# One activation table for exponential and logarithm, Silu by ACT's own function in one block a phase, and the convolution in u's slot

## The reference, cut to what matters

```python
x = einsum('ed,bld->bel', in_proj_w, ctx)
u = silu(causal_conv4(x) + conv_b)                      # 4 taps per channel
x_dbl = einsum('ke,bel->bkl', x_proj_w, u)              # dt_lo (16), B (16), C (16)
delta = softplus(einsum('er,brl->bel', dt_proj_w, dt_lo) + dt_proj_b)
state = state * exp(delta_t * A) + (delta_t * u_t) * B_t   # for each position t
y_t = sum_n state[.., n] * C_t[n]
y = (y + D * u) * silu(layernorm(X))
X = X + tanh(g_xattn) * y
h = layernorm(X)
X = X + tanh(g_ffn) * (top-2 gates of softmax(h Wr); sum over slots of gate * (h U) V)
```

## Time and profile before

| what | before |
|---|---|
| median of 3 runs | 543.68 us (542.85 to 543.94) |
| the profiled execution's own time | 542.47 us |
| its span, first to last instruction | 540.7 us |
| PE busy | 490.6 us, 91% |
| DVE busy | 477.4 us, 88% |
| POOL busy | 457.8 us, 85% |
| ACT busy | 392.0 us, 73% |
| mean granted TensorE clock | 0.981 |

### The profile page before, as it was taken

The page is one execution under the profiler, slowest core; times in us unless marked ns, Lnnn a source line. Parts: engine busy times, 40 slices in busy tenths (PEclk is TensorE's granted clock), DMA queues, the critical chain, the costliest instruction groups (busy, mean ns, idle before and its releaser), DMA issues.

```text
span 540.7 us, 9249 instructions
## 1 busy us (share of the span) xinstructions
PE 490.6 (91%) x3032; PEld 368.2 (68%) x3032; DVE 477.4 (88%) x880; ACT 392.0 (73%) x702; POOL 457.8 (85%) x338
## 2 busy tenths in 40 slices
PE   9979888988687999999998999999999999899688
PEld 5568787868476777658676777667657766676654
DVE  3698999979899999889999999888988989999852
ACT  4567779576867678587967878577888888888542
POOL 0399999969999998979999999989798898987810
PEclk9979999999998899999999999999999999999799
DMA  5495001045320001065130000086100000000001
GB/s 135 154 370 220 0 2 32 10 154 191 128 78 2 1 0 59 2 211 222 59 99 1 19 2 21 4 269 235 44 15 8 19 22 19 2 20 21 1 20 39
DMA packets 18705, 39.37 MB, mean 73 GB/s; under 512 B 5585, under 2 KB 6353, under 8 KB 18658
## 3 DMA queue, kind: packets, MB, share of 16 engines
q1 hardware_dynamic: 18658, 38.79, 21.1%
HBM read 34.33 MB, written 4.46 MB: 72 GB/s over the span
## 4 chain that ended last, share of the span: by engine, by line
PE 60%; DVE 17%; ACT 13%; issue 8%; POOL 1%; DVEq 0%; ACTq 0%; POOLq 0%
PE p_s L754 14%; PE p_y L776 12%; DVE state L1260 9%; PE p_v L809 9%; PE p_f L800 7%; PE p_tr L721 4%; PE p_pr L684 3%; ACT da L1011 3%; PE p_pr L696 2%; PE p_pr L677 2%; PE p_f L789 2%; PE p_y L825 1%; DVE p_s L1260 1%; ACT p_s L1011 1%; PE p_y L765 1%
## 5 line engine op out<-in xcount | busy, mean ns | idle before, releaser
L573 POOL TENSOR_TENSOR state<-state,c_bc 128x1024 f32<-128x1024 f32 (+1 forms) x131 | 256.7, 1972 | 20.2 <-DVE state L1260 17.9
L754 PEld LDWEIGHTS p_s<-pair_b,du_t 128*128 128x128 f32 x1072 | 138.8, 197 | 45.2 <-issue 31.5
L754 PE MATMUL p_s<-pair_b,du_t 128*128 128x128 f32 x1072 | 152.7, 284 | 16.2 <-DVE state L1260 14.1
L776 PE MATMUL p_y<-ident,state 128*128 128x128 f32 x1024 | 149.3, 276 | 0.0
L558 POOL TENSOR_TENSOR dbu<-du,pair_b 128x1024 f32<-128x1024 f32 (+1 forms) x80 | 145.3, 1819 | 1.5 <-DVE p_s L1260 1.5
L1011 ACT ACTIVATE p_s<-delta,a_neg 128x512 f32<-128x512 f32 (+1 forms) x162 | 93.6, 581 | 70.0 <-DVE state L1260 34.2
L1260 DVE TENSOR_TENSOR_SCAN state<-da,p_s 128x512 f32<-128x512 f32 (+1 forms) x116 | 134.2, 1170 | 6.5 <-PE p_s L754 6.1
L776 PEld LDWEIGHTS p_y<-ident,state 128*128 128x128 f32 x1024 | 121.4, 144 | 23.7 <-issue 21.2
L1011 ACT ACTIVATE da<-delta,a_neg 128x512 f32<-128x512 f32 (+1 forms) x158 | 100.4, 648 | 18.6 <-DVE state L1260 18.2
L1260 DVE TENSOR_TENSOR_SCAN state<-p_s,dbu 128x512 f32<-128x512 f32 (+1 forms) x100 | 98.1, 996 | 3.5 <-POOL dbu L558 3.5
L800 PE MATMUL p_f<-u_sb,h_t 128*128 128x512 f32 x112 | 56.8, 610 | 1.2 <-DVE gw L1363 1.2
(11 more groups left out here) (182 smaller groups left out, 680.7 us busy)
## 6 DMA issues: line engine op xcount, KB each, us to landing
c_bc<-bc_rows SPq DMA_DIRECT2D x32, 512.0 KB, 5.4
pair_b<-bc_rows SPq DMA_DIRECT2D x16, 512.0 KB, 6.0
xs<-in_x SPq DMA_DIRECT2D x16, 256.0 KB, 4.1
out<-ot SPq DMA_DIRECT2D x14, 256.0 KB, 2.0
cx<-in_ctx_t SPq DMA_DIRECT2D x4, 512.0 KB, 3.7
u_sb<-in_u_w SPq DMA_DIRECT2D x1, 1024.0 KB, 14.1
v_sb<-in_v_w SPq DMA_DIRECT2D x1, 1024.0 KB, 15.6
w_in<-in_in_w_t SPq DMA_DIRECT2D x1, 384.0 KB, 4.7
```

Of the source, the lines that this page charges most:

```text
L573: eng.tensor_tensor(pair, pair, c_bc[:, 2 * p:2 * p + 2, c0:c0 + w], ALU.mult).then_inc(po_cs, 1)
L754: mm = eng.matmul(p_s[g % BANKS][:, t * P:(t + 1) * P], du_t[:, f % 2, t, :], diagonals_of(n // 2)[:, n % 2, c0 // P + t, :], start=(t == ...
L776: mm = eng.matmul(p_y[:, t, :], slot(NS * f + n)[:, t * P:(t + 1) * P], ident[:, :], is_transpose=True, start=False, stop=(n == NS - 1 and ...
```

## The change

- **z**: ACT computes silu(z) directly (`silu_z` on ACT), and the factor tanh(g_xattn) moves into the copy of the transposed result (`copy_sz`, now with a scale). DVE's `silu_z` and the halving in POOL's `scale_of_z` (6 small instructions, now 4) go.
- **u**: the convolution is built up in u's own slot (`conv_v`), a ring of 5 slots for 6, and ACT's Silu works in place. `tanh_v` on ACT and `silu_u` on DVE go, and DVE's two scalings of the tap weights by 0.5.
- **The block**: once a phase ACT loads Silu's table, makes the Silus and loads the set that has both Exp and Ln. It stands at n = 9, behind `skip`, in phases 12 to 19 only in the even ones and for two phases' z; in phases 2, 6 and 10 it stands at n = 15 and has two blocks of u, since the next phase needs them.
- **Opening**: the diagonal matrices of pairs 6, 7 and 0 of batch 0 move from POOL to ACT, four instructions of two tiles each per pair, behind the decays of n = 2 to 13 of phase 0. The fillers between the small projections are 3, 2, 1, 2. The table load stands ahead of `copy_small`, no longer behind it.
- Waits follow: `conv_first` now waits for the slot of u (`ac_skip`, du), `dt_projection` and softplus for the taps and no longer for u.

```diff
-U_RING = 6
+U_RING = 5
@@
-        return b > 0 and p == pe_pairs(b)[-1]
+        return p == pe_pairs(b)[-1] or b == 0 and p in (0, 6)
@@
-            for k, count in enumerate((3, 2, 4, 6)):
+            for k, count in enumerate((3, 2, 1, 2)):
                 keep_clock(count)
                 small_projection(0, [k])
@@ scalar engine
+            def silu_z(f):
                 b, k, c0, w = PHASE[f]
+                eng.wait_ge(po_zs, ZOPS * (b + 1))
+                eng.wait_ge(s_x[b % 2][k], 16 * (b // 2 + 1))
+                before = f - 1 if f <= SPLIT else f - 2 - f % 2 + 1
+                if f:
+                    eng.wait_ge(pe_turn, TURN["sz", before] + 1)
+                eng.activation(zh_of(f), xs[:, b % 2, k, c0:c0 + w], ACT.Silu, bias=zr[:, b % 2, 1, k:k + 1],
+                               scale=zr[:, b % 2, 0, k:k + 1]).then_inc(ac_z, 1)
@@
             eng.wait_ge(po_k, 9)
+            eng.preload_act_table_set("natural_log_exp_and_others")
             copy_small(0)
-            eng.preload_act_table_set("natural_log_exp_and_others")
+            softplus(0, 0)
             copy_b(0)
-            softplus(0, 0)
             softplus(0, 1)
             softplus(0, 2)
@@ in the loop over f and n
+                ahead_of_turn = f + 1 < SPLIT and PHASE[f + 1][1] == Q - 1
+                    if f == 0 and n in (2, 3, 4, 5):
+                        diagonals(0, 6, n - 2)
+                    if f == 0 and n in (6, 7, 8, 9):
+                        diagonals(0, 7, n - 6)
+                    if f == 0 and n in (10, 11, 12, 13):
+                        diagonals(0, 0, n - 10)
@@
                     if n == 12 and f + 5 < BLOCKS:
                         conv_first(f + 5)
-                    if n == 13:
-                        z_part(f, 0)
-                    if n == 14:
-                        z_part(f, 1)
-                        if f == 0:
-                            tanh_v(4)
+                    if n == 15 and f < LAST:
+                        copy_du(f + 1)
+
+                    if n == (15 if ahead_of_turn else 9) and (f < SPLIT or f % 2 == 0):
+                        eng.preload_act_table(ACT.Silu)
+                        silu_z(f)
+                        if f >= SPLIT:
+                            silu_z(f + 1)
+                        for q in range(u_made, min(f + 5 + ahead_of_turn, BLOCKS)):
+                            silu_u(q)
+                        u_made = min(f + 5 + ahead_of_turn, BLOCKS)
+                        eng.preload_act_table_set("natural_log_exp_and_others")
                     if n == 15:
-                        if f < LAST:
-                            copy_du(f + 1)
-                        if f + 5 < BLOCKS:
-                            tanh_v(f + 5)
                         if Q <= f < EARLY + Q and f % Q:
                             normed(f - Q)
@@ vector engine
-            def silu_u(q):
-                eng.wait_ge(ac_th, q - Q + 1)
-                if q >= U_RING:
-                    eng.wait_ge(ac_skip, q - U_RING + 1)
-                eng.scalar_tensor_tensor(out=u[:, q % U_RING, :], in0=conv_bank(q)[:, :], scalar=1.0, in1=conv_v(q),
-                                         op0=ALU.add, op1=ALU.mult).then_inc(ve_u, 1)
```

More of the change, by code:

```diff
@@ L80, in flamingo @@
     POOL_TILES = [(f, p) for f in range(F) for p in pool_pairs(PHASE[f][0])]
-    DIAGONALS = [(0, p) for p in pe_pairs(0)[1:] + [0]]
+    DIAGONALS = [(0, p) for p in pe_pairs(0) if not by_act(0, p)]
+    ACT_DIAGONALS = [(0, 6), (0, 7), (0, 0)] + [(b, pe_pairs(b)[-1]) for b in range(1, B)]
     DIAGONALS += [(b, p) for b in range(1, B) for p in pe_pairs(b) if not by_act(b, p)]
@@ L151, in flamingo @@
         minus_half = sb("minus_half", [P, Q])
-        half = sb("half", [P, Q])
+        minus_one = sb("minus_one", [P, Q])
         a_neg = sb("a_neg", [P, Q, NS])
@@ L296, in conv_v @@
         def conv_v(q):
-            return x2[:, q // Q, q % Q, :] if q < 5 else vsp[:, :]
+            return x2[:, q // Q, q % Q, :] if q < 5 else u[:, q % U_RING, :]
         def close_place(T, which):
@@ L378, in wait_for_du, with zh_of @@
                 eng.wait_ge(ve_du, 1)
[L380 to L385, removed]
+        def zh_of(f):
+            c = PHASE[f][3] * (f % 2) if f >= SPLIT else 0
+            return zh[:, c:c + PHASE[f][3]]
         block = ctx.enter_context(nc.Block())
@@ L964, in softplus, with copy_turn @@
                     eng.activation(sp, sp, ACT.Ln, bias=1.0).then_inc(ac_sp, 1)
-            def copy_turn(kind, i, dest):
+            def copy_turn(kind, i, dest, scale=1.0):
                 eng.wait_ge(pe_turn, TURN[kind, i] + 1)
@@ L969, in copy_turn @@
                 bank = turn_bank(kind, i)
-                eng.activation(dest, bank[:, :, 0:NS] if kind == "b" else bank[:, 0:blocks, :], ACT.Copy).then_inc(ac_turn, 1)
+                eng.activation(dest, bank[:, :, 0:NS] if kind == "b" else bank[:, 0:blocks, :], ACT.Copy,
+                               scale=scale).then_inc(ac_turn, 1)
             def copy_b(b):
                 if b:
-                    if b > 1:
-                        eng.wait_ge(ac_diag, 2 * Q * (b - 1))
+                    eng.wait_ge(ac_diag, 2 * Q * (b + 2))
                     eng.wait_ge(po_diag, DIAGONALS.index((b, pe_pairs(b)[0])))
@@ L982, in copy_du, with diagonals @@
                 copy_turn("du", f, du_t[:, f % 2, 0:PHASE[f][3] // P, :])
-            def diagonals(b, part):
-                p = pe_pairs(b)[-1]
+            def diagonals(b, p, part):
                 n = 2 * p + part // 2
-                if part == 0:
+                if (b, p, part) == (0, 0, 0):
+                    eng.wait_ge(ve_dbu, 2)
+                if b == 0 and part == 0:
+                    eng.wait_ge(ac_turn, TURN["b", 0] + 1)
+                elif part == 0:
                     before = first_phase(b) - 1
@@ L1103, in _ @@
             conv_first(2)
-            silu_first(0)
+            silu_u(0)
             conv_first(3)
-            silu_first(1)
+            silu_u(1)
             eng.wait_ge(s_w, 16 * 5)
@@ L1456, in _ @@
                             f_statistics(T, 1)
-                        silu_z(f)
                         for T in stats[1:]:
                             f_statistics(T, 2)
-                    if f == 0 and n == 15:
-                        silu_u(4)
-                    if n == 15 and f + 5 < BLOCKS:
-                        silu_u(f + 5)
                     if (f, n) in c_by_dve:
```

109 lines of the change are left out of this document (37 added, 72 removed).

## The result

The changed kernel takes 550.77 us (median of 4 runs, 549.60 to 551.85), against 543.60 us for the kernel before on the same chip. The ratio is 1.0128 with a 95% interval of [1.0110, 1.0145]: it is slower by 1.3%. The forecast was 548.0 us with a range of 540 to 553.

The account below looks back on a forecast made before the run. It took DVE, POOL or PE as full by phase, ACT's in-order block as the risk. Terms summed to +1.9, with the clock +4.3: 546.8 on the profiled 542.47, 548.0 us against the 543.68 median; range 540 to 553.

Parts of the forecast that it names:

- The point that decides: Phases 6 and 10: `h` behind the block ends 3.9 us later, PE waits at `turn_h`; +3.9 and +3.4.
- The clock: Behind PE's two 5 us waits, phases 7 and 11: lower granted clock costs 1.2 us each, +2.4.
- Opening and phase 0: First scan 1.35 us earlier; first tap of block 5 waits, +1.9; DVE saves 1.7; phase 0 ends +0.2.
- The fillers' share: Opening: with 1 and 2 fillers for 4 and 6, the last small projection starts 1.35 us earlier.
- Phases 1 to 3: Phase 1 +0.2 (late tap +1.4, DVE -1.2), phase 2 nothing despite its late decay, phase 3 -0.6 from earlier delta.
- Phases 4, 5, 8 and 9: DVE saves 1.2 us each, `turn_h` input 0.5 earlier in 5 and 9, taps 0.3 to 0.8 late: -2.4.
- The last batch: Phases 12 to 19: DVE saves 0.4 us per phase; 0.33 taken for each of seven phases, -2.3.
- the first (faster, the block absorbed): PE's `turn_h`, phases 6 and 10: no late `h`, or phases 7 and 11 absorb it; 538.3 us, chance 0.19.
- The second: No change: the two delays cost 0.9 us less each and the clock stays up; 543.8 us, chance 0.12.
- The third, late taps in every phase: Phases 4, 5, 7, 8, 9: DVE waits 1.4 us for the first tap, PE idles; +5, 553 us, chance 0.09.
- The fourth, a load that drains ACT: ACT's table loads: each block costs 2.8 us more by the skill page's drain figure; chance 0.02.

Follow-up runs that it names:

- experiment 1: Changed kernel with the layernorm `h` made ahead of the Silu block in phases 6 and 10: 536.66 us, 0.9881 of the kernel before.
- experiment 5: Kernel before with three more ACT table loads right ahead of `h` in phases 6 and 10: 556.11 us, 1.0209 of the kernel before.
- experiment 2: Changed kernel with 14 filler products on PE ahead of the transposes of `h` in phases 6 and 10: 546.09 us, 1.0044 of the kernel before.
- experiment 6: Changed kernel with the opening's fillers as before, 3, 2, 4, 6 for 3, 2, 1, 2: 553.85 us, 1.0172 of the kernel before.
- experiment 12: Changed kernel, `h` and next phase's first decay ahead of the block in phases 2, 6, 10 where present, phase 0's block at n = 13: 534.74 us, 0.9858.
- experiment 8: Changed kernel with `h` ahead of the block in phases 6 and 10 and phase 0's block at n = 13: 533.81 us, 0.9808 of the kernel before.
- experiment 10: Changed kernel with a Silu block in every last-batch phase, two more loads in each odd one: 550.85 us, 1.0137 of the kernel before.
- experiment 11: Changed kernel with `h` first, phase 0's block at n = 13, and POOL making the diagonals of pairs 6, 7, 0 again: 532.71 us, 0.9807.
- experiment 9: Kernel before with DVE's `silu_z` left out in the eight last-batch phases: 543.50 us, 0.9996 of the kernel before.
- experiment 7: Changed kernel with one more 256-column DVE instruction in each of the eight last-batch phases: 555.75 us, 1.0203 of the kernel before.

## Why the forecast was right, and where its terms were off

**The point that decides** was named rightly, place, order and releaser: `h` is 4.06 us later behind du_t (forecast 3.9), PE waits 5.17 (forecast about 5), and experiments 1 and 5 show that this alone makes the kernel slower. Without it the change gains 1.2%. All of the delay reaches the end, in phase 10 as in phase 6. There the forecast had 3.4, since it credited phase 11 with 0.5 of PE's 2.7 us of idle time. Experiment 5 has the same 2.7 idle in a phase 11 that begins late: the waits behind this idle time move along with PE.

**The clock** was forecast as +1.2 at each place, and is +1.9 and +2.7 (experiment 2), +2.2 each in experiment 5. The estimate came from a stretch of 3.4 us; with waits of 5 us it is 6.8 us long and begins within the wait. PE works for only part of it, 4.0 and 5.6 us, and half of that is 2.0 and 2.8, nearly what was measured. In experiment 5's second stretch it is 4.5 us, and half is 2.3.

**Opening and phase 0** came to +0.7 for +0.2. The fillers' share is right (experiment 6), but the first scan starts only 0.86 us earlier and not 1.35, and this is the whole 0.5. Counted from the first scan phase 0 came as forecast: the tap is 20.2 us behind it (47.82 less 27.59; forecast 47.3 less 27.1, before 17.0), and the phase takes 28.6 us (forecast 27.0 and the 1.35 and 0.2). The forecast named only the wait at the tap, where DVE has two for one block, 2.52 us for the decay behind it and then 2.39. DVE's saving there, 1.6 for 1.7, is right. An error of 0.5 can't be told from chance here: three traces with the opening and phase 0 of before end this phase at 55.5, 56.6 and 58.1 us, five with those of the changed kernel at 56.2 to 58.9.

**Phases 1 to 3** came to -0.7 for -0.4, but laid out otherwise: phase 2 is 1.4 longer and phase 3 2.5 shorter. Experiment 12 moves the same 2.4 us across this boundary without changing the sum. That DVE's wait for the first decay costs nothing was right. **Phases 4, 5, 8 and 9**: -2.6 for -2.4, and that it fits so well is luck. Ten more traces are of programs that run the same in these phases as the changed kernel. Five of them have its 113.3 to 113.6 us; in the other five (experiments 1, 8, 10, 11 and 12) it is 112.2, and there the lower clock comes in phase 4 (granted clock 0.88 to 0.95) and leaves phase 5 at 0.99 or 1.00 and 27.2 us long, for 0.94 and 28.6 us in the changed kernel. Experiments 5 and 9, which run these phases as the kernel before does, have 117.0 and 117.2 for its 116.2. So the saving lies between 2.6 and 5.0.

**The last batch** was forecast at -2.3 and gave -0.6. The term that failed is "0.33 for each of seven phases, between 0 and 0.6", which took DVE's saving to pass nearly in full. Leaving out DVE's work alone gives 0.3 us (experiment 9), and two more loads on ACT in each odd phase cost nothing (experiment 10). An added DVE instruction does cost, 3.8 us in all (experiment 7), but one that POOL holds up: the phases in which it took 0.99, 0.67 and 0.55 us (12, 13 and 16) are 0.9, 0.6 and 0.5 longer. With 0.68 and 0.53 us in phases 14 and 15 it cost nothing; why wasn't tried. The 1.8 of phase 17 come ahead of its own added instruction: behind phase 16's, PE waits 1.47 us for DVE, 1.0 in the changed kernel, and the clock falls. What one more `silu_z` would cost stays open, and so does how much of a saving on DVE would reach the end if PE had more room.

Of the rivals, the first (faster, the block absorbed) needed PE to have room; it had none that counted. The second needed the clock to stay up; it fell. The third, late taps in every phase, didn't come: DVE waits 0.4 to 0.7 us for a tap in three later phases (1, 3 and 8), beside 2.39 in phase 0. In phase 1 the forecast had 1.4 for it, and 0.6 came. The fourth, a load that drains ACT, is ruled out: the instruction behind a load starts 1.29 us after the load does, in experiment 5 three times in a row.

The errors of the terms are +0.5, -0.3, -0.2, +1.0, +2.4 and +1.7 us in the table's order (phases 1 to 3 taken together), 5.1 in all on the profiles. All three large ones lie on the slow side. Against the medians only 2.8 of it shows (550.77 for 548.0), since the two profiled runs lie 1.1 on either side of theirs; that nearness is no merit of the sum.

## What to carry to other kernels

When work is gathered into one block on an engine that runs in order, list what stands behind the block and ask for each who waits for it: with that order mended the change gained 1.2% here, and one instruction of 0.8 us behind the block, which could as well stand ahead, cost 14 us in the traces, at two places. Of two engines that wait for each other in turn, idle time on either is not room: neither did PE's in phase 11 take up a delay, nor did less work on DVE in the last batch shorten it by more than 0.3 us. A wait that PE can't avoid is cheaper with something in it, as a third of this one's price was the clock behind it. To test what an instruction costs, add that same one: another with its inputs elsewhere can meet another engine.

## What the runs showed of the hardware

- **DVE and POOL hold each other up.** The first two products `dbu` on DVE, the same instructions in three programs, took 1.29 us together (experiment 5), 2.19 (before) and 2.72 (changed kernel), from the timelines of DVE. In the last two a POOL instruction of 128x1024 had started between them or before them (26.48 beside 26.34, and 24.54 ahead of 24.94). Before, DVE's first had started ahead of it and took 0.69 us, as in experiment 5, and the POOL instruction took 1.50 where the same one takes 1.09 in experiment 5. In experiment 5 POOL's small one beside them took 1.27 us instead of 0.31, and its large one started after them. So part of the opening's gain was lost: the first decay comes 1.53 us earlier in the changed kernel, the first scan 0.86. In experiment 7 a DVE instruction of 256 columns took between 0.27 and 0.99 us, and seven times of eight it ended 0.15 us after POOL's.
- **The lower clock also follows shorter waits**: 0.58 for 3.4 us in phase 17 of experiment 7, behind a wait of PE of 1.47 us, as behind the 1.49 us of the earlier trace rows.
- **A scale from a tile of its own costs ACT's copy 0.09 us**: `sz_t` takes 601 ns on average with it and 507 without, by the groups of the two kernels. The forecast had 0.1.
